# Four graph networks on one core: folded norms in the passages, a third network tile by tile, and fillers on TensorE

## What is computed

```python
h = jnp.maximum(_layernorm(x, axis=-1), 0.0)
x = x + _L0_gnn_ref(h, edge_index, batch0, ...)   # 7 layers, last step _ln(h, norm_g[6], norm_b[6])
h = jnp.maximum(_layernorm(x, axis=-1), 0.0)
x = x + _L1_gnn_ref(h, edge_index, node_vec1, ...) # 4 blocks: norm, attention, norm, two dense
h = jnp.maximum(_layernorm(x, axis=-1), 0.0)
x = x + _L2_gnn_ref(h, wc, wn, bias, edge_index)   # h @ wc + mean over edges of h @ wn + bias
h = jnp.maximum(_layernorm(x, axis=-1), 0.0)
x = x + _L3_gnn_ref(h, edge_attr_512, path_coeffs, src, dst, path_indices)

def _layernorm(x, axis=-1, eps=1e-05):
    m = jnp.mean(x, axis=axis, keepdims=True)
    v = jnp.var(x, axis=axis, keepdims=True)
    return (x - m) / jnp.sqrt(v + eps)
```

## Time and profile before

| | us |
|---|---|
| median of three runs | 954.59 |
| lowest, highest | 952.15, 957.04 |
| the profiled execution | 958.74 |
| its span in the trace | 956.9 |
| TensorE busy (share of the span) | 784.0 (82%) |
| VectorE busy | 608.1 (64%) |
| ScalarE busy | 226.7 (24%) |
| GpSimd busy | 141.7 (15%) |

### The profile page before, as it was taken

One profiled execution on the slowest core, in us unless ns is written; L12 is line 12 of the kernel. 1 busy time (PEld: TensorE's weight loads), 2 busy tenths in 40 slices (PEclk: granted clock), 3 DMA queues, 4 the chain that ended last, 5 costly groups with the idle time before them and its releaser, 6 DMA issues.

```text
span 956.9 us, 10169 instructions
## 1 busy us (share of the span) xinstructions
PE 784.0 (82%) x2802; PEld 500.9 (52%) x2802; DVE 608.1 (64%) x1562; ACT 226.7 (24%) x449; POOL 141.7 (15%) x153
## 2 busy tenths in 40 slices
PE   7287988978984999999999977126887998979998
PEld 3163554554552756766657543124465475565663
DVE  8463665655667353533543633178999999999980
ACT  6321120120221222222221311300420602406300
POOL 5000000000001000000010000720171081240000
PEclk9678999999996999999999999569998999999999
DMA  6703222322232224324333101820341344130000
GB/s 210 257 1 99 99 88 99 99 88 99 99 99 62 88 72 148 120 83 134 113 105 99 55 1 41 316 82 1 154 122 33 154 132 154 34 99 1 0 1 22
DMA packets 35905, 89.97 MB, mean 94 GB/s; under 512 B 3570, under 2 KB 3967, under 8 KB 35231
## 3 DMA queue, kind: packets, MB, share of 16 engines
q1 hardware_dynamic: 30752, 72.81, 22.0%
q0 software_dynamic: 5120, 16.78, 6.0%
HBM read 88.53 MB, written 1.05 MB: 94 GB/s over the span
## 4 chain that ended last, share of the span: by engine, by line
PE 35%; issue 29%; DVE 19%; DVEq 9%; SPq 3%; POOL 2%; DMA 2%; ACT 1%; POOLq 0%; ACTq 0%
PE PS L736 25%; DVE big L1323 6%; DVEq L1317 6%; PE PS L954 4%; DVE tail L1333 4%; PE PS L968 3%; POOL rstd L527 1%; DMA big<-_L_gnn_path_indices_dram 1%; DVE tail L1342 1%; DVE prods L1342 1%; DVEq L1323 1%; POOL big L547 1%; DVEq L1318 1%; PE PS L770 1%; DVE big L1096 1%
## 5 line engine op out<-in xcount | busy, mean ns | idle before, releaser
L1333 DVE SCALAR_TENSOR_TENSOR tail<-big,coef 128x448 f32 (+2 forms) x220 | 139.0, 634 | 1.5 <-issue 1.5
L736 PE MATMUL PS<-big 128*128 128x512 f32 (+1 forms) x368 | 136.2, 523 | 2.9 <-DVE big L1261 1.8
L1323 DVE TENSOR_TENSOR big<-big,tail 128x448 f32 (+2 forms) x220 | 127.0, 577 | 10.8 <-DVE tail L1333 5.1
L736 PEld LDWEIGHTS PS<-big 128*128 128x128 f32 x368 | 67.9, 190 | 65.8 <-issue 62.0
L527 POOL TENSOR_TENSOR rstd<-var,minus_half 128x1 f32<-128x1 f32 x38 | 28.7, 764 | 472.9 <-DVE var L1010 472.9
L547 POOL DMA_INDIRECT big<-h_rows,src_i x64 | 85.0, 1328 | 83.8 <-PE PS L954 60.6
L736 PE MATMUL PS<-hT,big 128*128 128x256 f32 x384 | 84.9, 381 | 4.2 <-ACT hT L648 4.2
L736 PEld LDWEIGHTS PS<-hT,big 128*128 128x128 f32 x384 | 72.3, 190 | 15.5 <-issue 3.9
L954 PE MATMUL PS<-big,hotd_more 128*128 128x512 f32 x176 | 76.3, 592 | 0.0
L1028 DVE TENSOR_TENSOR h<-PS,h 128x512 f32<-128x512 f32 x26 | 17.9, 689 | 79.7 <-PE PS L736 79.7
L968 PE MATMUL PS<-xn,tail 128*128 128x256 f32 x104 | 30.5, 445 | 40.8 <-issue 27.2
(11 more groups left out here) (184 smaller groups left out, 1067.0 us busy)
## 6 DMA issues: line engine op xcount, KB each, us to landing
big<-in_L_gnn_vn_W_dram SPq DMA_DIRECT2D x12, 1024.0 KB, 5.3
big<-in_edge_attr_dram SPq DMA_DIRECT2D x3, 3584.0 KB, 10.7
big<-in_L_gnn_m_w_dram SPq DMA_DIRECT2D x8, 1024.0 KB, 5.3
big<-in_L_gnn_gcn_W_dram SPq DMA_DIRECT2D x7, 1024.0 KB, 5.3
big<-in_L_gnn_wv_dram SPq DMA_DIRECT2D x4, 1024.0 KB, 5.3
big<-in_L_gnn_wq_dram SPq DMA_DIRECT2D x4, 1024.0 KB, 5.2
big<-in_L_gnn_wk_dram SPq DMA_DIRECT2D x4, 1024.0 KB, 5.4
big<-in_L_gnn_wo_dram SPq DMA_DIRECT2D x4, 1024.0 KB, 5.4
```

Of the source, the lines that this page charges most:

```text
L736: return pe.matmul(o, lhsT, rhs, start=start, stop=stop)
L1323: dve.tensor_tensor(o, o, prod[:, row % RING, 0:n, :], ALU.add)._wait_ge(path_step, g * STEPS + 2 * row + 1).then_inc(path_step, 1)
L1333: dve.scalar_tensor_tensor(out=prod[:, row % RING, 0:n, :], in0=xs[:, :, bass.ds(i1, EXT)], scalar=coef[:, row:row + 1], in1=xe[:, :, bass ...
```

## The change

The passages are rewritten.

First passage, VectorE: gain is multiplied onto h minus mean in one pass, and root and x follow in one pass; the bias is added to x already in the first layer. The second norm isn't written out any more: h becomes max(x - mean, 0) without its root. The third norm, which is taken of h, makes up for it in its variance: `first_var` puts LN_EPS times the variance of x in place of LN_EPS, so that one root serves, and the missing root (rstd_in) is multiplied onto h after both tiles of xn are written. TensorE gets eleven fillers before the tables, six behind them, and one between the tiles (FILL_L1_IN); the tables wait for the statistics of x instead of the second norm.

Second network: `turn_y` moves from the start of a block to the end of the one before.

Second passage: each tile is normalised right behind its last residual; transposition, clip and products go tile by tile.

Third passage: subtraction of the mean and maximum in one pass, then the root.

```diff
-FILL = 6
+FILL, FILL_L1_IN = 6, (11, 6, 1)
@@ GpSimd
-            inverse_root(LN_L1_IN)
+            inverse_root(LN_L1_IN, var_in, rstd_in)
@@ ScalarE
-            for b in turned(TR_L2):
-                act.activation(hT[:, 2 * b:2 * b + 2, :], chunks(0)[:, 2 * b:2 * b + 2, :], ACT.Relu, bias=zero).then_inc(yT_ready, 1)
+            for t in range(NT):
+                act.wait_ge(tr_done, TR_L2 * 2 + (t + 1))
+                act.activation(hT[:, :, t * P:(t + 1) * P], turned_tile(t), ACT.Relu, bias=zero).then_inc(yT_ready, 1)
@@ TensorE
             def block1(b, last):
-                turn_y(b * 2, 2)
...
                 dense(0, mT, 2, down_done, None, 0)
-
-            pe.wait_ge(ln_out, LN_L1_IN * 2 + 2)
+                if not last:
+                    turn_y(b * 2 + 2, 2, FILL)
+
+            keep_busy(3, FILL_L1_IN[0])
+            pe.wait_ge(st_set, LN_L1_IN * 2 + 2)
             for t in range(NT):
                 table(0, 0, t)
+            keep_busy(3, FILL_L1_IN[1])
+            turn_y(0, 2, FILL_L1_IN[2])
...
-            turn(TR_L2, ln_out, OUT_L2 * 2)
+            turn_tile(0)
             pe.wait_ge(w_in[3], 16 * (BLOCKS + 1))
-            dense(2, hT, 3, beta_done, yT_ready, 4 * BLOCKS)
+            dense_tile(2, 3, 0, beta_done)
+            turn_tile(1)
             pe.wait_ge(w_in[5], 32 * (BLOCKS + 1))
-            dense(4, hT, 5, alpha_done, None, 0)
+            dense_tile(4, 5, 0, alpha_done)
+            dense_tile(2, 3, 1, beta_done)
+            dense_tile(4, 5, 1, alpha_done)
@@ VectorE, first layer
+                    dve.wait_ge(gb_in, 32)
+                    for t in range(NT):
+                        ins = dve.tensor_tensor(x[:, t, :], x[:, t, :], gb[:, 1, :], ALU.add)
+                    link(ins)
@@ VectorE, first passage
-            layer_norm(LN_L0_LAST, h)
-            dve.wait_ge(ln_out, LN_L0_LAST * 2 + 2)
-            dve.wait_ge(gb_in, 32)
-            for k, op in ((0, ALU.mult), (1, ALU.add)):
-                for t in range(NT):
-                    ins = dve.tensor_tensor(xn[:, t, :], xn[:, t, :], gb[:, k, :], op)
-                link(ins)
-            link(dve.tensor_tensor(x[:], x[:], xn[:], ALU.add))
-
-            take_stats(x)
-            layer_norm(LN_L1_IN, x)
-            dve.wait_ge(ln_out, LN_L1_IN * 2 + 2)
-            link(dve.tensor_scalar(h[:], xn[:], 0.0, None, ALU.max))
-            take_stats(h)
+            for t in range(NT):
+                aggregate(LN_L0_LAST, t)
+            for t in range(NT):
+                link(dve.scalar_tensor_tensor(out=xn[:, t, :], in0=h[:, t, :], scalar=mv[:, t, 0:1],
+                                              in1=gb[:, 0, :], op0=ALU.subtract, op1=ALU.mult))
+            for t in range(NT):
+                dve.wait_ge(ln_est, LN_L0_LAST * 2 + (t + 1))
+                link(dve.scalar_tensor_tensor(out=x[:, t, :], in0=xn[:, t, :], scalar=rstd[:, t:t + 1],
+                                              in1=x[:, t, :], op0=ALU.mult, op1=ALU.add))
+                stats(t, x).then_inc(st_set, 1)
+            for t in range(NT):
+                dve.wait_ge(st_set, LN_L1_IN * 2 + (t + 1))
+                link(dve.bn_aggr(mv[:, t, :], st[:, t, :]))
+                dve.tensor_scalar(var_in[:, t:t + 1], mv[:, t, 1:2], LN_EPS, None, ALU.add).then_inc(ln_var, 1)
+                link(dve.tensor_scalar(h[:, t, :], x[:, t, :], mv[:, t, 0:1], 0.0, ALU.subtract, ALU.max))
+                stats(t, h).then_inc(st_set, 1)
+
+            def first_var(t):
+                dve.wait_ge(st_set, LN_BLOCK * 2 + (t + 1))
+                link(dve.bn_aggr(mv[:, t, :], st[:, t, :]))
+                dve.scalar_tensor_tensor(out=var[:, t:t + 1], in0=var_in[:, t:t + 1], scalar=ln_eps,
+                                         in1=mv[:, t, 1:2], op0=ALU.mult, op1=ALU.add).then_inc(ln_var, 1)
...
             for t in range(NT):
-                cond_norm(0, t)
+                cond_norm(0, t, first_var)
+            for t in range(NT):
+                dve.wait_ge(ln_est, LN_L1_IN * 2 + (t + 1))
+                ins = dve.tensor_scalar(h[:, t, :], h[:, t, :], rstd_in[:, t:t + 1], None, ALU.mult)
+            link(ins)
@@ VectorE, second passage
                     residual(t, 0, down_done, b * 2, x if last else h)
-                    if not last:
+                    if last:
+                        aggregate(LN_L2, t)
+                        normalise(LN_L2, t, x)
+                    else:
                         cond_norm(b * 2 + 2, t)
...
-            layer_norm(LN_L2, x)
@@ VectorE, third passage
-            layer_norm(LN_L3, x)
-            dve.wait_ge(ln_out, OUT_L3 * 2 + 2)
-            for t in range(NT):
-                dve.tensor_scalar(h[:, t, :], xn[:, t, :], 0.0, None, ALU.max).then_inc(h_ready, 1)
+            for t in range(NT):
+                aggregate(LN_L3, t)
+                link(dve.tensor_scalar(xn[:, t, :], x[:, t, :], mv[:, t, 0:1], 0.0, ALU.subtract, ALU.max))
+            for t in range(NT):
+                dve.wait_ge(ln_est, LN_L3 * 2 + (t + 1))
+                dve.tensor_scalar(h[:, t, :], xn[:, t, :], rstd[:, t:t + 1], None, ALU.mult).then_inc(h_ready, 1)
```

More of the change, by code:

```diff
@@ L936, in _, with turn_tile, dense_tile @@
             block1(BLOCKS - 1, True)
-            turn(TR_L2, ln_out, OUT_L2 * 2)
+            def turn_tile(t):
+                pe.wait_ge(ln_out, OUT_L2 * 2 + (t + 1))
+                for c in range(CT):
+                    ins = pe.transpose(turned_tile(t)[:, c, :], xn[:, t, c * P:(c + 1) * P], ident[:])
+                ins.then_inc(tr_done, 1)
+            def dense_tile(bank, i, t, done):
+                pe.wait_ge(yT_ready, 4 * BLOCKS + (t + 1))
+                for c in range(CT):
+                    ins = mm(PS[:, bank + t, :], hT[:, c, t * P:(t + 1) * P], wbuf[i][:, c, :], c == 0, c == CT - 1)
+                ins.then_inc(done, 1)
+            turn_tile(0)
             pe.wait_ge(w_in[3], 16 * (BLOCKS + 1))
-            dense(2, hT, 3, beta_done, yT_ready, 4 * BLOCKS)
+            dense_tile(2, 3, 0, beta_done)
+            turn_tile(1)
             pe.wait_ge(w_in[5], 32 * (BLOCKS + 1))
-            dense(4, hT, 5, alpha_done, None, 0)
+            dense_tile(4, 5, 0, alpha_done)
+            dense_tile(2, 3, 1, beta_done)
+            dense_tile(4, 5, 1, alpha_done)
             pe.wait_ge(beta_ready, 2)
@@ L1020, in layer_norm, with normalise @@
                 for t in range(NT):
[L1021 to L1023 removed]
+                    normalise(n, t, inp)
+            def normalise(n, t, inp):
+                dve.wait_ge(ln_est, n * 2 + (t + 1))
+                dve.tensor_scalar(xn[:, t, :], inp[:, t, :], mv[:, t, 0:1], rstd[:, t:t + 1],
+                                  ALU.subtract, ALU.mult).then_inc(ln_out, 1)
             def residual(t, bank, done, value, to):
@@ new lines, in first_var, with cond_norm @@
+            def first_var(t):
[3 more added lines that the diff above has]
+                                         in1=mv[:, t, 1:2], op0=ALU.mult, op1=ALU.add).then_inc(ln_var, 1)
+            def cond_norm(k, t, variance=None):
+                if variance is None:
+                    aggregate(k + LN_BLOCK, t)
+                else:
+                    variance(t)
```

22 lines of the change are left out of this document (9 added, 13 removed).

## The result

The changed kernel took 943.16 us (median of four runs, 942.5 to 946.96), the kernel before 953.87 in four runs beside it (952.15 to 957.04). The ratio is 0.9892, with a 95% interval of 0.9854 to 0.993: 10.3 us faster, 6.7 to 13.9 by the interval. On two other occasions the same program gave ratios of 0.9878 (0.984 to 0.9917) and 0.9884 (0.9854 to 0.9915), with medians of 945.33 and 945.38.

What follows compares the result with a forecast made beforehand. No engine owns the chain of waits; passages between networks, where VectorE, GpSimd and TensorE take turns, lie on the path in full. 6.85 + 4.35 + 0.3 = 11.5 us off the median 954.59 gives 943.1, range 939.0 to 948.0.

Steps and rivals of the forecast that it cites:

- First passage, VectorE: Between first and second network: VectorE's shorter chain of norms writes tile 1 at 305.6 instead of 308.94, 3.3 us earlier.
- First passage, TensorE: Second network's first product at 306.7 instead of 313.55: 6.85 us, 3.3 from VectorE and 3.5 from fillers out of the way.
- Rival (a): TensorE's clock falls in the first passage after all, in a gap: 2.1 us lost, 945.2 us; chance 20%.
- the argument from the gaps: First passage: TensorE's gaps of 1.9, 1.6 and 1.3 us are shorter than 3.01, so the clock is taken as held.
- Second passage: Between second and third network: first product 3.55 us earlier, transposes 0.5 back, full-clock products 1.3 more; sum 4.35 us.
- Third passage: Before the fourth network: maxima and roots change places, ending at 595.2 instead of 595.55; 0.3 us taken, ends 0 and 0.5.
- the term of 0.05: Third passage's gain if the one-input max pass does not slow GpSimd's root, by the skill page; the sum 0.25 less.
- First layer: Two bias additions, 1.38 us, fit into VectorE's 1.41 us of idle time: at nothing, at most 1.4 us.
- Block edge: Turning of y moved to a loop turn's end: nothing taken, bounds 0 to 0.3 us at each of three edges.
- rival (d): Slower: TensorE's code reload at loop edges is no longer hidden; at 4 us each 959.1 us; chance 3%.
- (b): First passage: clock already low at 291.4, so fillers stand in the way; gain 2.65 instead of 6.85, 947.3 us; chance 4%.
- (c): Second network's first block: the earlier start meets another wait, only the second passage's gain stays; 949.95 us; chance 6%.

Runs made afterwards that it cites:

- e7: The changed kernel with 15, 9 and 3 fillers in the first passage in place of 11, 6 and 1: 948.61 us.
- e9_more_fill_again: The changed kernel with 15, 9 and 3 fillers once more, beside the changed kernel on the same chip: 942.95 us against 945.38.
- e3: The kernel before with only TensorE's first-passage part, with more fillers (20, 10, 1), and the moved turning of y: 958.28 us, ratio 1.0001.

## Why the prediction was right, step by step

- **First passage, VectorE.** Tile 1 was forecast 3.3 us earlier; from the second variance it came 3.9 earlier (11.6 in place of 15.5). The prices held: max pass 0.48 (forecast 0.50), two-tensor passes 0.75. The statistics overlap with the next aggregation by 0.08 us, which I had counted at full length.
- **First passage, TensorE.** Forecast 15.3 us from product to product, measured 14.8 in every trace with the change. "I take the clock as held" was a coin's throw and not a likelihood of three to one: the clock fell at a place that costs 1.7 us in two of five traces. Rival (a) priced it right (1.7 in the products; the 0.4 in the transposes didn't come, since it fell behind them), and its 20% was too low. The step that failed there is the argument from the gaps: I compared each gap of 1.3 to 1.9 us with the 3.01 of the earlier trace rows and concluded that the clock holds. With gaps of 1.7, 1.1 and 1.2 us it fell in four of the five traces with these fillers, in two of them at no cost and in two at 1.7 us in the second network; with the gaps filled (e7, e9_more_fill_again) it fell in none of two. What decides it is not shown.
- **Second passage.** Forecast 4.35, measured 4.4 against the first trace of before, and 4.2 to 5.9 over all. Every intermediate number held: root 0.55, tile 0 ready 0.3 us before it is asked for (forecast 0.3), 1.7 us of cover for tile 1, full clock. First product 1.3 us after the last one (1.4 forecast).
- **Third passage.** Forecast 0.3, measured 0.36. The max pass slows a root, to 0.72 and 0.87, less than the 0.99 beside two tensors. The rule of the Trainium skill (GPSIMD Engine Reference, 1. Specifications) agrees with the trace in its direction if the max pass counts as one in a two-port mode, which no trace shows; the term of 0.05 that I worked out by it was too low. The prediction missed a row of the kernel before that bears on it: there the second root of a norm (593.52), beside the pass with two columns, took 0.65.
- **First layer.** At nothing, as forecast: the two additions took 1.28 us and left 0.17 of idle time in front of the second bias addition. From the start of an earlier pass of VectorE (63.83 in the kernel before, 63.75 in the changed one) to that of this second addition it is 8.7 us in all fourteen traces, nine of them with the two additions and five without. VectorE's timeline of the changed kernel:

```profile
67.86 1.28 DVE L1189 TENSOR_TENSOR x<-x,big 128x512 f32<-128x512 f32 x2
...
72.46 0.69 DVE L1199 TENSOR_TENSOR h<-PS,tail 128x512 f32<-128x512 f32 x1 [0.17 <-PE PS L737]
```

- **Block edge, and rival (d).** The second network takes 254.08 with the moved turning (e3) and 254.07 to 254.11 without. Nothing, as forecast.
- **Rivals (b) and (c).** The clock was full when the first fillers began (22 records in 4.91 us), and no new wait came up in the first block.
- **The sum.** Means over the traces: passage one 21.6 to 14.8, the second network +0.7, passage two (five traces of the old order) 20.4 to 15.5, the third 8.03 to 7.67, in all 11.4; forecast 11.5, measured 10.3 (interval 6.7 to 13.9). The clock's 0.7, which I had left out, was made up by a second passage that is worse in the kernel before, on average, than in its one trace. That is luck, and so is the median that was met to 0.1 us: the kernel before ran 0.7 lower beside the change than in the runs that the forecast stood on, and the changed kernel itself took 945.3 and 945.4 on the two other occasions. The rewritten pieces are what the forecast had right.

## What to carry to other kernels

Where a passage between two engines' stretches is on the path, price every hand-over and every pass by its row and add them up: here that gave each rewritten piece to within half a microsecond of the first pair of traces; it did not give the clock behind them. Look at fillers as work that can stand in somebody's way: put them where the engine waits for something known to be late, and few of them ahead of the tile that ends the wait. And cut two traces at the same events before explaining their difference: 5.9 of the 16.2 us here lay in code that was not changed.

## What the runs showed of the hardware

- The clock's fall is not a function of the kernel alone: with TensorE's program the same, and its idle pieces ahead of the fall the same to 0.1 us, it fell 7.7 us after the first network's last product, 15.6 after it, or not at all. The first network's end lies anywhere between 289.8 and 296.1, and the more time TensorE had spent at half clock until then (37.5 to 58.0 us), the later it is. Why it is at half clock for longer in one execution than in another is not shown.
- VectorE's passes in the fourth network's first group stop for 1.3 to 3.0 us, at the same instruction, in five traces (61.5 to 61.8 for the group) and not in six others (56.2 to 56.5). In three traces the group took 57.2 to 58.8. The position of VectorE's own code was excluded as the cause; the gathers are left as a candidate that one trace fits.
- A root of one column on GpSimd takes 0.55 us with VectorE idle, 0.72 and 0.87 beside the max pass, which has one tensor and one column, 0.65 beside a pass with one tensor and two columns, and 0.99 beside one with two tensors.
